# A recommender tower on one core: layer 2 summed on VectorE in place of TensorE, a third PSUM bank for ScalarE, loops written out

## The reference, cut to what matters

```python
e = jnp.stack([tbl_0[ids[:, 0]], ...], axis=1)          # [512, 32, 32]
prev = e; outs = []
for W in (filter_0, filter_1):
    z = jnp.einsum('bhd,bmd->bhmd', e, prev)            # products of two fields
    cur = jax.nn.relu(jnp.einsum('bpd,pn->bnd', z, W))  # 128 maps
    prev = cur; outs.append(cur)
z = jnp.sum(jnp.concatenate(outs, axis=1), axis=-1)     # summed over the 32 numbers
h = jnp.maximum(jnp.concatenate([z, dense_ctx], axis=1) @ W_top1 + b_top1, 0.0)
h = jnp.maximum(h @ W_top2 + b_top2, 0.0)
y = h @ W_top3
```

## Time and profile before

| what | value |
|---|---|
| median of 3 runs | 876.31 us (875.47 to 878.77) |
| the profiled execution: time, span | 873.6 us, 871.8 us |
| TensorE busy | 864.0 us (99%) |
| VectorE busy | 796.5 us (91%) |
| ScalarE busy | 681.2 us (78%) |
| GpSimd busy | 674.7 us (77%) |
| granted TensorE clock, mean | 0.996 |

### The profile page before, as it was taken

The page is one execution under the profiler, slowest core; times in us unless marked ns, Lnnn a source line. Parts: engine busy times, 40 slices in busy tenths (PEclk is TensorE's granted clock), DMA queues, the critical chain, the costliest instruction groups (busy, mean ns, idle before and its releaser), DMA issues.

```text
span 871.8 us, 17386 instructions
## 1 busy us (share of the span) xinstructions
PE 864.0 (99%) x3587; PEld 672.7 (77%) x3587; DVE 796.5 (91%) x2393; ACT 681.2 (78%) x2231; POOL 674.7 (77%) x677
## 2 busy tenths in 40 slices
PE   7999999999999999999999999999999999999998
PEld 3777787777787777778777778777777877777875
DVE  4888999989998999999999999999999998999983
ACT  3778878778887877887877888787788787888873
POOL 5577689777977887878878797987979787786680
PEclk9999999999999999999999999999999999999999
DMA  5788856776766577775757676576766677673330
GB/s 171 189 201 181 197 100 157 161 168 159 170 143 134 147 172 164 171 175 100 163 139 183 159 168 167 103 169 153 183 158 147 131 161 164 158 183 72 74 73 0
DMA packets 55038, 129.97 MB, mean 149 GB/s; under 512 B 8036, under 2 KB 19268, under 8 KB 55013
## 3 DMA queue, kind: packets, MB, share of 16 engines
q0 software_dynamic: 22240, 68.17, 43.3%
q1 hardware_dynamic: 31090, 58.74, 21.1%
q10 hardware_dynamic: 1683, 2.80, 1.0%
HBM read 59.43 MB, written 4.20 MB: 73 GB/s over the span
## 4 chain that ended last, share of the span: by engine, by line
PE 94%; DVE 2%; DMA 2%; issue 1%; ACT 1%; POOL 0%; SPq 0%; DVEq 0%; ACTq 0%
PE t_act L793 14%; PE t_act L795 13%; PE t_act L794 13%; PE t_dve L793 13%; PE t_dve L795 13%; PE t_dve L794 13%; PE acc L761 6%; PE acc L766 4%; PE acc_pool L803 1%; PE acc L770 1%; PE acc_pool L805 1%; DMA x_rows<-emb 1%; DVE prod L576 1%; DVE prod L587 0%; PE t_act L879 0%
## 5 line engine op out<-in xcount | busy, mean ns | idle before, releaser
L419 ACT ACTIVATE prod<-t_act,weigh 128x128 f32<-128x128 f32 x2048 | 577.5, 372 | 117.2 <-PE t_act L795 115.5
L576 DVE SCALAR_TENSOR_TENSOR prod<-t_dve,weigh,prod 128x128 f32<-128x128 f32 x1792 | 481.5, 340 | 11.1 <-PE t_dve L795 7.1
L304 POOL TENSOR_TENSOR prod<-prod 128x512 f32<-128x512 f32 (+1 forms) x255 | 321.2, 1260 | 18.3 <-DMA prod<-prod 8.3
L793 PE MATMUL t_act<-w_hi,cur_hi 128*128 128x512 f32 x512 | 215.9, 422 | 0.0
L286 POOL DMA_DIRECT2D prod<-prod x126 | 118.8, 943 | 106.9 <-DVE prod L576 72.9
L795 PE MATMUL t_act<-w_hi,cur_lo 128*128 128x512 f32 x512 | 200.1, 391 | 0.0
L794 PE MATMUL t_act<-w_lo,cur_hi 128*128 128x512 f32 x512 | 200.0, 391 | 0.0
L793 PE MATMUL t_dve<-w_hi,cur_hi 128*128 128x512 f32 x512 | 199.9, 390 | 0.0
L795 PE MATMUL t_dve<-w_hi,cur_lo 128*128 128x512 f32 x512 | 199.6, 390 | 0.0
L794 PE MATMUL t_dve<-w_lo,cur_hi 128*128 128x512 f32 x512 | 199.5, 390 | 0.0
L267 POOL DMA_INDIRECT emb<-table_dram,all_ids x128 | 158.2, 1236 | 40.3 <-issue 26.9
(11 more groups left out here) (98 smaller groups left out, 609.5 us busy)
## 6 DMA issues: line engine op xcount, KB each, us to landing
prod<-prod POOLq DMA_DIRECT2D x126, 512.0 KB, 5.0
x_shift<-x_rows SPq DMA_DIRECT2D x62, 512.0 KB, 6.1
x_pair<-x_rows SPq DMA_DIRECT2D x94, 128.0 KB, 4.7
x_same<-x_rows SPq DMA_DIRECT2D x31, 256.0 KB, 3.5
x_rows<-emb SPq DMA_DIRECT2D x64, 64.0 KB
w_raw<-w_dram ACTq DMA_DIRECT2D x8, 256.0 KB, 4.8
emb<-table_dram,all_ids POOLq DMA_INDIRECT x128, 2.8
w_raw<-wt_dram SPq DMA_DIRECT2D x2, 512.0 KB, 7.2
```

The source lines that it names most:

```text
L304: nc.gpsimd.tensor_tensor(src[:, dst, :], src[:, dst, :], src[:, other, :], ALU.add).then_inc(folded, 1)
L419: last = nc.scalar.activation(prod[i][:, HEADS * k + j, :], t_act[k % ARING][:, j * MAPS:(j + 1) * MAPS], ACT.Copy, scale=weigh[p][:, i, h ...
L576: nc.vector.scalar_tensor_tensor(dst, src, w, dst, ALU.mult, ALU.add).then_inc(added, 1)
L793: nc.tensor.matmul(bank[:, :], cur_hi[p][:, cols], w_hi[:, w], start=True, stop=False)
```

## The change

Layer 2's sum over the 32 numbers leaves TensorE. ScalarE rectifies `side` into `cur2` in fp32. VectorE turns it in blocks of 32 by 32 and sums along the row (`sum2`), which gives for each chunk 16 columns of a small array `pool2`. `lower2`, `place`, `pooling`, the copy of `acc_pool2` and the 4 transposes are gone. At the end TensorE brings `pool2` into the tower's layout with a matrix of ones, `pick`: `turn_sums` is 16 matmuls in fp32, once for the first 31 chunks (124 columns each) and once for the last (4 columns each). The bank that `acc_pool2` held becomes a third bank for ScalarE. `pooling1` moves behind tile 3. The tower's first product now waits for all of VectorE's banks, and three of the four context products come ahead of it. A table `ORDER` says which banks of a tile are ScalarE's and which VectorE's; it is `EVEN` for every tile, that is the same 4 and 4 as before. The hardware loops are gone: every chunk is written out.

```diff
+EVEN = "ADADADAD"
+ORDER = [FULL if False else EVEN for tile in range(CHUNKS * TILES)]
-DRING, ARING = 4, 2
+DRING, ARING = 4, 3
...
-        def over_chunks(eng, chunk, head=2, tail=2, after_head=None):
+        def over_chunks(chunk, cut=CHUNKS, between=None):
...
-            with eng.Fori(head // 2, (CHUNKS - tail) // 2) as pair:
-                for parity in range(2):
-                    chunk(pair * 2 + parity, parity)
-            for c in range(CHUNKS - tail, CHUNKS):
+            for c in range(cut, CHUNKS):
                 chunk(c, c % 2)
...
-                nc.scalar.activation(cur2_hi[p][:, :, :], side[p][:, :, :], ACT.Relu).then_inc(cur2_hi_ready, 1)
+                nc.scalar.activation(cur2[p][:, :], side[p][:, :, :].rearrange("x i n -> x (i n)"), ACT.Relu
+                                     ).then_inc(cur2_ready, 1)
...
-            def lower2(c, p):
...
-            def place(c, p):
...
+            def sum2(c, p):
+                dve.wait_ge(cur2_ready, c + 1)
+                wait(dve, pool2_ready, c)
+                nc.vector.transpose(turned2[:, :], cur2[p][:, :]).then_inc(cur2_turned, 1)
+
+                dve.wait_ge(cur2_turned, c + 1)
+                nc.vector.tensor_reduce(pool2[:, :, :, c].rearrange("x h i -> x i h"),
+                                        turned2[:, :].rearrange("x (i h d) -> x i h d", i=TILES, d=DIM),
+                                        AX.X, ALU.add).then_inc(pool2_ready, 1)
...
                 add_tile(c, 2, p)
                 if more1:
                     lower(c + 1, 1 - p)
-                    pooling1(c + 1, 1 - p)
-                lower2(c - 1, 1 - p)
+                sum2(c - 1, 1 - p)
                 add_tile(c, 3, p)
                 if more2:
                     products(c + 2, p, 1)
+                if more1:
+                    pooling1(c + 1, 1 - p)
...
-                if not first:
-                    pooling(c - 1, 1 - p)
...
+            def turn_sums(chunks):
+                to = t_act[0].rearrange("n (i c q) -> n i c q", i=TILES, q=QUARTERS)
+                for q in range(QUARTERS):
+                    for h in range(MAPS // DIM):
+                        left = PICK - 128 - h * DIM
+                        last = nc.tensor.matmul(to[:, :, chunks, q], pick[:, q, left:left + 128], pool2[:, h, :, chunks],
+                                                start=h == 0, stop=h == MAPS // DIM - 1)
+                return last
...
-                pe.wait_ge(added, (CHUNKS * TILES * HALF - DRING + f + 1) * HEADS)
+                pe.wait_ge(added, D_UPTO[-1] * HEADS)
...
-            top_ctx(0)
-            top_ctx(1)
+            for f in range(3):
+                top_ctx(f)
+            pe.wait_ge(weighed, A_UPTO[-1])
+            pe.wait_ge(pool2_ready, CHUNKS - 1)
+            turn_sums(slice(0, CHUNKS - 1))
             warm_up(HOLD_UPS, acc1)
-            pooling(CHUNKS - 1, (CHUNKS - 1) % 2)
-            top_ctx(2)
...
+            pe.wait_ge(pool2_ready, CHUNKS)
+            turn_sums(slice(CHUNKS - 1, CHUNKS)).then_inc(pool2_turned, 1)
             top_ctx(3)
```

More of the change, by code:

```diff
@@ L22 @@
 BANKS = FIELDS // HEADS
-HALF = BANKS // 2
-FEEDS = HALF * HEADS
-DRING, ARING = 4, 2
-SEL_WIDE = 2 * 128 - QUARTERS
+EVEN = "ADADADAD"
+FULL = "ADAADADA"
+ORDER = [FULL if False else EVEN for tile in range(CHUNKS * TILES)]
+A_BANKS, D_BANKS = ([order.count(who) for order in ORDER] for who in "AD")
+A_UPTO, D_UPTO = ([sum(banks[:tile]) for tile in range(CHUNKS * TILES + 1)] for banks in (A_BANKS, D_BANKS))
+DRING, ARING = 4, 3
+PICK = 2 * 128 - DIM
 CTX, TOP1, TOP2 = 16, 512, 256
@@ L31 @@
 W_PIECE = FIELDS * MAPS // W_PIECES
-HALVE = (slice(0, 8), slice(8, 16))
-FOLDS = [(slice(0, 4), slice(4, 8)), (slice(0, 2), slice(2, 4))]
+FOLDS = {8: [(slice(0, 4), slice(4, 8)), (slice(0, 2), slice(2, 4))],
+         10: [(slice(0, 5), slice(5, 10)), (slice(0, 2), slice(2, 4)), (slice(0, 1), slice(4, 5))]}
+HALVES = [banks * HEADS // 2 for banks in A_BANKS]
+FOLDED = [sum(len(FOLDS[half]) for half in HALVES[:tile]) for tile in range(CHUNKS * TILES + 1)]
 COLD_UPS = 7
@@ L78, in dlrm_tower @@
         w_lo = sb("w_lo", [128, FIELDS * MAPS], f32r)
-        prod = [sb(f"prod{i}", [128, FEEDS, MAPS]) for i in range(TILES)]
+        prod = [sb(f"prod{i}", [128, 2 * max(HALVES[i::TILES]), MAPS]) for i in range(TILES)]
         side = [sb(f"side{p}", [128, TILES, MAPS]) for p in range(2)]
@@ L293, in fold @@
                 tile = c * TILES + i
-                done = tile * len(FOLDS)
+                half = HALVES[tile]
+                done = FOLDED[tile]
                 if halve_here:
-                    pool.wait_ge(weighed, (tile + 1) * HALF)
-                    pool.wait_ge(added, (tile + 1) * FEEDS)
+                    pool.wait_ge(weighed, A_UPTO[tile + 1])
+                    pool.wait_ge(added, D_UPTO[tile + 1] * HEADS)
                 else:
                     pool.wait_ge(halved[i % 2], (c * (TILES // 2) + i // 2 + 1) * 16)
-                for step, (dst, other) in enumerate([HALVE] * halve_here + FOLDS):
+                steps = [(slice(0, half), slice(half, 2 * half))] * halve_here + FOLDS[half]
+                for step, (dst, other) in enumerate(steps):
                     if step > 0:
@@ L827, in chunk @@
             def chunk(c, p):
-                fixed = isinstance(c, int)
-                more = not (fixed and c + 1 >= CHUNKS)
-                first = fixed and c == 0
+                more = not (c + 1 >= CHUNKS)
+                first = c == 0
                 layer2(c, 0, p)
@@ L936 @@
     spread = spread.reshape(128, 1 + GROUPS, 128)
+    pick = np.zeros((128, QUARTERS, PICK), np.float32)
+    for q in range(QUARTERS):
+        for l in range(DIM):
+            pick[q * DIM + l, q, PICK - 128 + l] = 1.0
     arrays = {
```

162 lines of the change are left out of this document (65 added, 97 removed).

## The result

The changed kernel takes 865.86 us, the median of 3 runs (865.07 to 866.52), against 876.31: a ratio of 0.989, 95% interval 0.9866 to 0.9914. The forecast was 864.6 in a range of 858.5 to 871. The profiled execution took 865.07 us with a span of 863.3, 8.5 less than before. By spans the forecast was further off than by medians: the sum gave 860.05, and 863.3 came. The median of before lay 2.7 us above its profiled execution, that of after only 0.8, and that hides 1.9 of the 3.2 us; that the median came so near is luck to that extent.

A forecast was written before the change was run, and what follows sets the result against it. TensorE, busy 99% of the span, was taken as the bound. -13.95 (pooling) - 5.1 (third bank) + 7.3 (end) = -11.75 us gave 861.9 for the profiled execution and 864.6 us for the median, range 858.5 to 871.

The forecast's parts named there:

- Pooling, 13.95 us: TensorE behind tile 3: two pooling matmuls, 0.45 us, gone in 31 chunks, all on the path, 13.95 us less.
- the third bank, 5.1: TensorE's wait for ScalarE's third bank of tile 3 goes: 30 x 0.17 = 5.1 us less.
- The loops, nothing: Hardware loops written out: the turns cost TensorE nothing, so nothing was taken for their absence.
- VectorE, nothing: VectorE's edits in each chunk: 1.44 us removed, 1.35 added; it stays second, 24.4 us of a chunk, costed at nothing.
- the 0.27 in the sum of the latter: Subtracted in forecasting how far VectorE starts tile 0 behind TensorE: 2.98 + 0.62 + 0.60 - 0.27 = 3.9.
- The rival that VectorE becomes the bound: Dearer transpose and stretches put VectorE at 25.5 us a chunk, 10.8 us back, 875 us; chance 0.08.
- The end, +7.3 us: TensorE's chain behind VectorE's last product until ScalarE reads the turned sum: 16.0 us, 7.3 more than before.
- 1.8 us either way: Clock at the end: same loss as before, with 1.8 us, half a 3.5 us stretch, to either side.
- A pass, 0.13 us: Each small fp32 pass at the end, 124 or 4 columns, priced at 0.13 us; 32 passes take 4.16 us.
- passes that are free: Rival at the end: passes of 4 columns nearly free, the lower price holds, about 860.3 us; chance 0.13.
- dear at 0.41: Rival at the end: small passes do not hide their weights, 64 take 26.4 us instead of 8.3, 882.7 us; chance 0.06.
- Three side sums of the prediction: End 3.0 more with lower pass prices; 863.0 us by the skill's load price; 11.7 us eaten at 0.31 a pass.

The follow-up runs named there:

- run 1: The changed kernel with two banks for ScalarE again, the third unused; 869.72 us, ratio 0.9932 to the kernel before.
- run 3: The kernel before with the second of its two pooling matmuls left out (low part of layer 2's result missing); 867.39 us, ratio 0.9919.
- run 2: The kernel before with its hardware loops written out and nothing else changed; 873.1 us, ratio 0.9988.
- run 4: The changed kernel with three more 128x512 transposes a chunk on VectorE, into tiles nothing reads; 893.06 us, ratio 1.0204.
- run 5: The changed kernel with one more 128x512 transpose a chunk on VectorE, into a tile nothing reads; 867.2 us, ratio 0.9898.
- run 9: The changed kernel, end reordered: 31 chunks' sums first, tower's first product bank by bank, two context products, last sums, two context products; 861.01 us.
- run 10: run 9 with 32 columns of weights for the small passes, each product writing its own 32 partitions without accumulation; 857.13 us, ratio 0.9795.
- run 6: The changed kernel with the tower's first product waiting bank by bank, not for all of VectorE's products at once; 860.51 us, ratio 0.9839.
- run 7: The changed kernel with 8 `warm_up` matmuls keeping TensorE busy ahead of the wait of the tower's first product; 864.4 us, ratio 0.9875.
- run 12: run 10 with all four context products ahead of the last sums and three 512-column matmuls right behind those sums; 853.51 us, ratio 0.9748.

## Why the prediction was right, point by point

- **Pooling, 13.95 us, and the third bank, 5.1.** Right in size and place: 0.62 us of a chunk gone, 0.17 by run 1, and 0.22 for one pooling matmul by run 3.
- **The loops, nothing.** Right, by run 2.
- **VectorE, nothing.** Right in its effect. The transpose costs 0.70 us as taken, the sum 0.69 for 0.68, steady as forecast. Its load was put at 24.4 us of a chunk, 97% of a window; it is 94.34%, 23.7 us. What was not foreseen lies in lines that the change left alone: in the groups of VectorE's lines the mean of L539 fell from 844 to 704 ns, of L524 from 931 to 746, of L530 from 752 to 720, which makes some 0.4 of the 0.7 us. For L539 the traces show why: before, 12 of its 32 instances began while an addition of GpSimd's was running and took over 0.9 us, as in run 4; now 2 do. The prediction had left these lines at their old cost. How far VectorE runs behind TensorE was right too: it starts tile 3 at 399.45 and tile 0 at 405.53, TensorE at 396.26 and 401.70, so 3.2 and 3.8 us for 3.3 and 3.9 (though the 0.27 in the sum of the latter names no row). The rival that VectorE becomes the bound was right in kind: with one line more it is nearly there (run 5), with three it is (run 4), and its spare time doesn't shrink by the added lines alone.
- **The end, +7.3 us, is the term that was mis-sized: it measures +11.2.** Its order was right (a chain behind VectorE's last product, in the order given); its clock was not. ScalarE reads the sum 18.2 us behind that product, for 16.0: the 12 matmuls took 4.50 for 2.72, the passes of 124 columns 5.22 for 4.16, those of 4 columns 3.56 (842.21 to 845.77) for 4.16, the rest as taken; 1.78 + 1.06 - 0.60 = 2.2. Behind the sum come another 1.6 us (863.3 - 845.88 = 17.4 for 15.8): the context product and the 12 matmuls of L855 and L871 ran at half clock, the latter 0.42 apart, to 852.85. The prediction had allowed the clock 1.8 us either way, half a stretch of 3.5; there were three stretches at half clock, one behind the pause (828.7 to 832.3 us, in the 12 matmuls), one behind the context products (835.6 to 839.0), one behind the passes of 4 columns (845.9 to 852.7), some 13.8 us. As an estimate from these figures, 10.3 us more at half clock lose 5.1, and passes that cost 0.111 in place of 0.13 at full clock give back 64 x 0.019 = 1.2: together the 3.9 us that the end is longer than forecast.
- **A pass, 0.13 us.** At full clock both kinds cost 0.111 (run 9, 124 columns; the profile after, 4 columns), so with 128 columns of weights what is moved doesn't count; where the clock was at half for a part of them, 0.163 on the mean of 32. That both blocks together took 8.78 us for the 8.3 forecast is luck: one was too long by the clock, the other too short by the price. The Trainium skill, "TensorE: Matmul & The Clock Gate", section LDWEIGHTS, by which 128 columns are an estimate of 0.107 us, is the better price here: the trace agrees at full clock, 0.111. By the same rule 32 columns would be an estimate of 0.027; run 10 shows 0.031 with 124 moved columns, near it, and 0.011 with 4, well under it. The rivals with passes that are free, or dear at 0.41, are both out. Three side sums of the prediction are a tenth or two off (3.1 for 3.0 more with the lower prices, 863.1 for 863.0, 11.5 for 11.7); nothing rests on them.

## What to carry to other kernels

Where one engine never rests, price a removed instruction by the distance of two starts: that held to 0.3 us of 19. The tail is another matter: there the clock fell behind a pause, behind context products of 16 rows and behind passes of 4 columns, so give each wait there a price in clock too, and let it wait for what it needs alone (5.4 us in run 6). Filling a gap with full matmuls gave 1.7 us of the end in run 7 and at most 0.6 in run 12, which the times alone don't confirm. And a matmul that moves few columns costs no less than one that moves 124 while it loads 128 columns of weights: load only those that are not zero. That, with partitions of their own, made the passes 3.6 and 10 times cheaper here. Last, when VectorE is nearly full, look at what GpSimd does beside it: a line moved in time can cost twice as much.

## What the runs showed of the hardware that was not expected

- The clock falls to 1.2 GHz without a pause just ahead: in run 9 it is granted 1.00 to 838 us, through 32 passes of 124 and most of 32 of 4 columns, and 0.58 in the 6 us behind, where TensorE was busy throughout with those passes and context products of 16 rows. In runs 6 and 7 TensorE made no pause either, and the clock fell behind the context products, in the passes of 124 columns (5.2 and 5.1 us for 32); in run 9 the same passes stood ahead of the context products and kept the full clock (3.56 us). A pause of 1.9 us was followed by a fall in two profiles of the changed kernel, pauses of 1.72 and 2.44 us in runs 1 and 5 were not, in the matmuls right behind.
- Passes with 32 columns of weights, each group written to other partitions, cost a tenth of those with 128 where 4 columns are moved (0.36 us against 3.56 for 32 passes), more than the factor of 4 in columns, and 0.99 us against 3.56 where 124 are.
- A VectorE line with two operands in SBUF went from a median of 0.68 us to 1.04 and 1.47 when one and three transposes of 0.7 us were put into the chunk behind it, though nothing in the line changed. All its instances over 0.9 us (12 before, 2 in the changed kernel, 22 and 26 in these runs) began while an addition of GpSimd's was running and ended 0.55 to 0.56 us behind that addition's end. The transposes beside it, with one operand, stayed at 0.66 to 0.71 us in both runs.
